# Ranking edges with first places in the last row of the marks, and 16-bit marks and frames laid out by fours in the first deal

## The reference

```python
h = relu(layernorm(x)); x = x + L0(h)   # mean of h[src] over the edges of each dst, then two 128x128 products
h = relu(layernorm(x)); x = x + L1(h)   # per-type weighted sums over dst, three products
h = relu(layernorm(x)); x = x + L2(h)   # attention with 4 heads over the edges of each src, with edge attributes
h = relu(layernorm(x)); x = x + segment_sum(h[dst], src)
```

## Time and profile before

| | us |
|---|---|
| median of 3 runs (11649.42 to 11655.3) | 11650.15 |
| the profiled execution | 11690.42 |
| its span | 11688.7 |
| second ranking loop, turn 0, inside 91 to 265 | 174 |
| second ranking loop, turn 1, inside 341 to 515 | 174 |
| first deal, 556 to 1250 | 694 |
| from 1260 to 11680 | 10420 |

### The profile page before, as it was taken

One profiled execution on the slowest core, in us unless ns is written; L12 is line 12 of the kernel. 1 busy time (PEld: TensorE's weight loads), 2 busy tenths in 40 slices (PEclk: granted clock), 3 DMA queues, 4 the chain that ended last, 5 costly groups with the idle time before them and its releaser, 6 DMA issues. The chain is left out here.

```text
span 11688.7 us, 111903 instructions
## 1 busy us (share of the span) xinstructions
PE 6256.4 (54%) x29027; PEld 4853.4 (42%) x29027; DVE 6469.5 (55%) x14870; ACT 2647.0 (23%) x8519; POOL 6742.7 (58%) x7099
## 2 busy tenths in 40 slices
PE   8744577777775355555554455555555333333333
PEld 2233455555554333333333455555555333333333
DVE  7799766666664455555554555555555622233223
ACT  0033111111110244444442243444444300000000
POOL 0055566666665566666665455555555466666665
PEclk6555788888887676666666777877777655555555
DMA  0000233333334422222222333333333322222223
GB/s 26 12 10 10 56 76 73 76 76 76 76 75 86 110 46 46 47 47 46 47 46 31 85 85 87 87 87 87 86 87 88 65 46 47 48 47 47 47 47 53
DMA packets 1413627, 706.78 MB, mean 60 GB/s; under 512 B 1170036, under 2 KB 1273944, under 8 KB 1412872
## 3 DMA queue, kind: packets, MB, share of 16 engines
q0 software_dynamic: 254160, 559.07, 19.0%
q1 hardware_dynamic: 1158840, 140.57, 8.6%
HBM read 595.05 MB, written 104.05 MB: 60 GB/s over the span
## 5 line engine op out<-in xcount | busy, mean ns | idle before, releaser
L1042 POOL DMA_INDIRECT l_rows<-h_tab,l_index x1616 | 1525.7, 944 | 942.3 <-issue 452.8
L1425 POOL DMA_INDIRECT l_rows<-h_tab,l_index x1616 | 1527.7, 945 | 868.5 <-issue 472.5
L603 POOL DMA_INDIRECT l_rows<-h_tab,l_words x1616 | 1524.6, 943 | 828.2 <-issue 461.8
L646 PE MATMUL l_sums<-l_onehot,l_rows 128*128 128x128 f32 x3232 | 829.5, 438 | 1599.0 <-issue 875.5
L1560 PE MATMUL l_sums<-l_weighted,l_rows 128*128 128x256 f32 x3232 | 1199.0, 537 | 712.7 <-DVE acc L1487 673.6
L646 PEld LDWEIGHTS l_sums<-l_onehot,l_rows 128*128 128x128 f32 x3232 | 719.6, 328 | 1708.9 <-issue 1076.1
L1947 PE MATMUL l_ps_q<-qtab,h 128*128 x3232 | 831.4, 413 | 1099.6 <-ACT h L1836 783.9
L634 DVE TENSOR_TENSOR acc<-acc,l_sums 128x128 f32 x1616 | 462.6, 286 | 1646.4 <-remote 733.8
L1439 ACT ACTIVATE l_weighted<-l_onehot,l_weights 128x128 f32<-128x128 bf16 x3232 | 987.5, 388 | 1427.2 <-DVE l_onehot L554 1084.1
L1487 DVE TENSOR_TENSOR acc<-acc,l_sums 128x256 f32 x1616 | 677.4, 419 | 1047.8 <-remote 687.4
L759 PE MATMUL src_sums<-tmp 128*128 128x288 f32 x3128 | 1042.2, 486 | 401.8 <-DVE tmp L736 217.7
(11 more groups left out here) (345 smaller groups left out, 11296.6 us busy)
## 6 DMA issues: line engine op xcount, KB each, us to landing
staged<-tmp SPq DMA_DIRECT2D x391, 152.0 KB
l_rows<-h_tab,l_index POOLq DMA_INDIRECT x3232
l_rows<-h_tab,l_words POOLq DMA_INDIRECT x1616
by_src<-words_src SPq DMA_DIRECT2D x96, 152.0 KB
l_kv<-kv_tab,l_words POOLq DMA_INDIRECT x816
l_attr<-in_edge_attr SPq DMA_DIRECT2D x44, 272.0 KB
l_kv<-kv_tab,moments POOLq DMA_INDIRECT x600
h_tab<-h SPq DMA_DIRECT2D x21, 448.0 KB, 3.0
```

The costliest lines, as they stand in the source:

```text
L603: pool.indirect_dma_start(rows[b][:, j, :], None, table, bass.IndirectOffsetOnAxis(ap=words[k % 3][:, at + j, 0:1], axis=0)).then_inc(rows ...
L646: done = nc.tensor.matmul(sums[q % SUMS][:, j, 0:P], rows[b][:, j, :], onehot[b][:, j, :], start=True, stop=True)
L1042: pool.indirect_dma_start(rows[b][:, j, 0:D], None, table, bass.IndirectOffsetOnAxis(ap=index[q // Q16 % WORDS][:, q % Q16 * H + j, :], ax ...
L1425: pool.indirect_dma_start(rows[b][:, j, :], None, h_tab, bass.IndirectOffsetOnAxis(ap=index[q // Q16 % WORDS][:, q % Q16 * H + j, :], axis ...
```

## The change

Ranking, second loop. The row 127 of each mask no longer holds a mask. It is overwritten by a DMA of the row of `start` for this bin, and `before` gets ones in its last row, so that one matmul adds both parts: four matmuls a bin in place of eight. Masks, `before`, `twice` and `zeros16` become float16, there are BINS_AHEAD = 4 masks, two of them in room of `h`, and `offer` and copy_predicated run on 127 rows. The edges of row 127 are placed apart: PE picks their bins (`from_last`), DVE makes `row_eq` and `row_sel` from them and from `row_value`, and at the end of the loop eight matmuls (`last_row`, `last_lift`) and one addition over 32 partitions (`tail`) bring their places into `chunk`.

First deal. `chunk`, `first` and `opened` are copied once to bfloat16, padded; a table of numbers 1 to 128, each repeated four times, is made by POOL, and DVE copies its bits into the PSUM table. Marks become `[P, GB, P, GC]` and frames `[BINS, P, GB]`: the innermost run is four neighbouring columns or deals of one number. Operands and output of these comparisons are then 16-bit values with step one. PE reads weights with a step of four elements (8 bytes).

```diff
+BINS_AHEAD = 4
+BLOCKS = -(-DEALS // GB)
+PADDED = BLOCKS * GB + 4
...
+                for turn in range(2):
+                    sp.wait_ge(start_ready, turn + 1)
+                    for b in range(NB):
+                        t = b % BINS_AHEAD
+                        if b >= BINS_AHEAD:
+                            sp.wait_ge(mask_used, turn * NB + b - BINS_AHEAD + 1)
+                        sp.dma_start(onehot[t][P - 1:P, :], start[b:b + 1, :]).then_inc(start_row_ready[t], 16)
                 sp.wait_ge(zeroed, ZEROS)
...
+                keep_where(before[:], ALU.not_equal, 1.0, 1 - P, [[0, P]])
+                for table, value in ((last_row, 1.0), (last_lift, K - 1.0)):
+                    ch.link(nc.gpsimd.memset(table[:], 0.0))
+                    ch.link(nc.gpsimd.memset(table[0:NB, P - 1:P], value))
...
-                ch.link(nc.gpsimd.memset(only[:], 0.0))
-                keep_where(only[:], ALU.not_equal, 1.0, 0, [[-1, BINS]])
...
+                    ch.link(nc.vector.scalar_tensor_tensor(by_group(start[:]), of_group, float(K), by_group(cnt), ALU.mult, ALU.add))
+                    nc.vector.scalar_tensor_tensor(by_group(row_value), of_group, float(K), by_group(run), ALU.mult, ALU.add).then_inc(start_ready, 1)
...
                     def offer(b):
-                        nc.vector.tensor_scalar(onehot[b % 2][:], bins_of[:], bins[:, b:b + 1], None, ALU.is_equal).then_inc(oh_ready[b % 2], 1)
+                        nc.vector.tensor_scalar(onehot[b % BINS_AHEAD][0:P - 1, :], bins_of[0:P - 1, :], bins[0:P - 1, b:b + 1], None,
+                                                ALU.is_equal).then_inc(mask_ready, 1)
...
+                    for b in range(BINS_AHEAD):
+                        offer(b)
+                    dve.wait_ge(row_bins_ready, turn + 1)
+                    dve.wait_ge(start_ready, turn + 1)
+                    ch.link(nc.vector.tensor_scalar(row_eq.rearrange("p (c q) -> p c q", c=4), banks[0][0:BINS, :, 0:CQ], bin_no[:, 0:1], None,
+                                                    ALU.is_equal))
+                    nc.vector.tensor_tensor(row_sel, row_value, row_eq, ALU.mult).then_inc(row_sel_ready, 1)
...
+                    dve.wait_ge(row_found, turn + 1)
+                    tail = chunk[P - 32:P, :].rearrange("p (c q) -> p c q", c=4)
+                    ch.link(nc.vector.tensor_tensor(tail, banks[1][P - 32:P, :, 0:CQ], tail, ALU.add))
...
+                    pe.wait_ge(row_sel_ready, turn + 1)
                     for b in range(NB):
...
+                        pe.wait_ge(mask_ready, turn * NB + b + 1)
+                        served = len(range(t, NB, BINS_AHEAD))
+                        pe.wait_ge(start_row_ready[t], 16 * (turn * served + b // BINS_AHEAD + 1))
                         if n:
                             pe.wait_ge(slot_used[s], turn * SERVED[s] + n)
                         for c in range(4):
-                            nc.tensor.matmul(banks[s][:, c, 0:CQ], before[:], onehot[s][:, cut], start=True, stop=False)
-                            last = nc.tensor.matmul(banks[s][:, c, 0:CQ], only[:, b:b + 1].to_broadcast([BINS, P]), start[:, cut], start=False, stop=True)
-                        last.then_inc(oh_used[s], 1)
+                            last = nc.tensor.matmul(banks[s][:, c, 0:CQ], before[:], onehot[t][:, c * CQ:(c + 1) * CQ], start=True, stop=True)
+                        last.then_inc(mask_used, 1)
+                    pe.wait_ge(slot_used[1], (turn + 1) * SERVED[1])
+                    for c in range(4):
+                        nc.tensor.matmul(banks[1][:, c, 0:CQ], last_row[:], row_sel[:, cut], start=True, stop=False)
+                        last = nc.tensor.matmul(banks[1][:, c, 0:CQ], last_lift[:], row_eq[:, cut], start=False, stop=True)
+                    last.then_inc(row_found, 1)
...
+    def lay(self, dve):
+        nc = self.nc
+        for to, of, n in ((self.chunk16, self.chunk, EC), (self.first16, self.first, DEALS + 1), (self.opened16, self.opened, DEALS)):
+            nc.vector.tensor_copy(to[:, 0:n], of[:, 0:n]).then_inc(self.laid, 1)
+            nc.vector.memset(to[:, n:], 0.0).then_inc(self.laid, 1)
+        dve.wait_ge(self.numbered, 1)
+        numbers = self.numbers[:].rearrange("p j c -> p (j c)").bitcast(F32)
+        nc.vector.tensor_copy(self.words_of_numbers, numbers).then_inc(self.laid, 1)
+        dve.wait_ge(self.laid, 7)
...
-        iota = self.iota[0:BINS, :].unsqueeze(1).to_broadcast([BINS, n, P])
-        of = lambda table, at: table[:, at:at + n].unsqueeze(2).to_broadcast([BINS, n, P])
-        nc.vector.tensor_tensor(self.left[b][:, 0:n, :], iota, of(self.opened, lo), ALU.is_equal)
+        iota = self.iota16[0:BINS, :, :]
+        of = lambda table, at: table[:, at:at + GB].unsqueeze(1).to_broadcast([BINS, P, GB])
+        nc.vector.tensor_tensor(self.left[b][:], iota, of(self.opened16, lo), ALU.is_equal)
...
+    def mark_chunks(self, m, lo, n):
+        size = [P, GB, P, GC]
+        chunks = self.chunk16[:, lo * GC:(lo + GB) * GC].rearrange("p (g c) -> p g c", c=GC)
+        self.nc.vector.tensor_tensor(self.onehot[m % 2][:], self.iota16.unsqueeze(1).to_broadcast(size), chunks.unsqueeze(2).to_broadcast(size),
+                                     ALU.is_equal)
+
+    def onehot_of(self, m, column):
+        return self.onehot[m][:, column // GC, :, column % GC]
+
+    def framed_of(self, table, i):
+        return table[:, :, i]
```

More of the change, by code:

```diff
@@ L256, in rank_phase @@
         start = sb("start", [BINS, EC], F16)
+        last_row, last_lift, bin_no = sb("last_row", [BINS, P], F16), sb("last_lift", [BINS, P], F16), sb("bin_no", [BINS, 1])
+        from_last = sb("from_last", [P, BINS], BF16)
+        halves_of_a = room[0:BINS, 2 * EC:3 * EC].bitcast(F16)
+        row_eq = halves_of_a[:, 0:EC]
+        row_value, row_sel = room[0:BINS, 0:EC], room[0:BINS, 3 * EC:4 * EC].bitcast(F16)[:, 0:EC]
         bins = sb("bins", [P, BINS])
-        only = sb("only", [BINS, BINS], F16)
-        twice = sb("twice", [P, 2 * BINS], BF16)
+        twice = sb("twice", [P, 2 * BINS], F16)
         lower = sb("lower", [BINS, BINS])
@@ L682, in wide @@
             return room[:, at:at + n].rearrange(f"p ({' '.join(names)}) -> p {' '.join(names)}", **dict(zip(names[1:], sizes[1:])))
-        self.onehot = [wide(f"onehot{b}", [span * GC, P]) for b in range(2)]
+        if dt != BF16:
+            self.onehot = [wide(f"onehot{b}", [span * GC, P]) for b in range(2)]
         self.filled = [wide(f"filled{b}", [span * GC, K * carried]) for b in range(2)]
@@ L686, in __init__ @@
         self.out = [wide(f"out{r}", [K, carried + self.ints]) for r in range(RING)]
-        frame = lambda name: sb(name, [BINS, GB, P], BF16)
-        self.left, self.next = ([frame(f"{name}{b}") for b in range(2)] for name in ("left", "next"))
+        if dt != BF16:
+            frame = lambda name: sb(name, [BINS, GB, P], BF16)
+            self.left, self.next = ([frame(f"{name}{b}") for b in range(2)] for name in ("left", "next"))
         ps = lambda name: own.enter_context(nc.psum_tensor(f"{tag}_{name}", [P, 512], F32))
@@ L751, in tensor @@
                 pe.wait_ge(self.move_kept, g)
-            nc.tensor.matmul(self.moves[:, 0:P], self.left[k][:, i, :], self.next[k][:, i, :], start=True, stop=True).then_inc(self.moved, 1)
+            nc.tensor.matmul(self.moves[:, 0:P], self.framed_of(self.left[k], i), self.framed_of(self.next[k], i),
+                             start=True, stop=True).then_inc(self.moved, 1)
         if g >= 2:
@@ L758, in tensor @@
         for c in range(GC):
-            last = nc.tensor.matmul(sums, self.onehot[m][:, at + c, :], self.filled[m][:, at + c, :].rearrange("p (k w) -> p k w", k=K),
+            last = nc.tensor.matmul(sums, self.onehot_of(m, at + c), self.filled[m][:, at + c, :].rearrange("p (k w) -> p k w", k=K),
                                     start=(c == 0), stop=(g == 0 and c == GC - 1))
@@ L809, in __init__, with number @@
         self.shift, self.trash = shift, trash
-        frame = lambda name: own.enter_context(nc.sbuf_tensor(f"{tag}_{name}", [BINS, GB, P], BF16))
+        sb16 = lambda name, shape: own.enter_context(nc.sbuf_tensor(f"{tag}_{name}", list(shape), BF16))
+        frame = lambda name: sb16(name, [BINS, P, GB])
+        self.left, self.next, self.closed = ([frame(f"{name}_of{b}") for b in range(2)] for name in ("left", "next", "closed"))
         self.begun, self.beyond = frame("begun"), frame("beyond")
-        self.closed = [frame(f"closed{b}") for b in range(2)]
+        self.onehot = [sb16(f"onehot_of{b}", [P, GB, P, GC]) for b in range(2)]
+        self.numbers = sb16("numbers", [P, P, GC])
+        self.chunk16, self.first16, self.opened16 = sb16("chunk16", [P, BLOCKS * GB * GC]), sb16("first16", [BINS, PADDED]), sb16("opened16", [BINS, PADDED])
         self.rows = own.enter_context(nc.sbuf_tensor(f"{tag}_rows", [P, RING], I32))
```

(11 more changed lines are left out.)

78 lines of the change are left out of this document (47 added, 31 removed).

## The result

After the change the median is 11542.67 us (4 runs, 11536.17 to 11552.14), before it is 11649.78 in the same comparison: a ratio of 0.9908, 95% interval 0.9895 to 0.992. The kernel is 107 us faster; 268 were forecast, and the time lies outside the range. The profiled execution of after has a span of 11534.4.

What follows compares the result with a forecast made beforehand. PE was taken to bound the ranking loop and DVE the first deal, POOL after the change. Ranking -79.2, deal -188.9 and +0.5 for its start sum to -267.6 us: median 11382.5 us, range 11362 to 11482.

Steps and rivals of the forecast that it cites:

- Ranking, -79.2: Second ranking loop, both turns: four matmuls fewer a bin, DVE sets the pace at 2.53 us, less additions: -79.2 us.
- Rows of `start`, 0: Ranking loop: PE's added wait for 49 single-row DMAs a turn stays hidden in 8.3 us of room, costing 0.
- rival 4: Ranking loop: rows of `start` land late, 12.3 us, so the loop gains nothing; 11481 us, chance 0.05.
- DVE's block, 4.93: First deal: 16-bit marks and frames at 0.52 ns an element cut DVE's block from 7.07 to 4.93 us.
- Rival 1: First deal: 16-bit comparisons reading PSUM don't run at twice the rate, block stays 7.07 us; 11573 us, chance 0.10.
- Strided weights: First deal: PE's weight loads of every fourth 16-bit element keep full speed; PE with ACT stays 0.77 us a deal.
- rival 2: First deal: strided weight loads slow PE, doubled loads giving 11511 us; case covers 11420 to 11573, chance 0.08.
- rival 3: First deal: strided loads far slower, four times the duration, whole kernel slower than before, about 12170 us; chance 0.03.
- Their second sign: First deal: DVE and POOL both idle for PE, named beside weight loads over 0.2 us as showing rivals 2 or 3.
- What is late next. POOL: First deal becomes bound by POOL's indirect DMAs, 1.27 us apart; first to last issue 685.4 to 496.5 us, -188.9.
- The ring: First deal's four output buffers: landing stays hidden, 3.3 us against 5.09 until the same buffer's turn.
- I see no path but the clock: The 10420 us of unchanged work after the first deal would not move by themselves, except through the clock.

Runs made afterwards that it cites:

- rank_alone: Only the change's ranking half, first deal as in before; median 11611.27 us, ratio to before 0.9925.
- flat16: The changed kernel with 16-bit operands kept but marks and frames laid out row by row again; median 11614.3 us, ratio to before 0.9929.
- laid32: The changed kernel with the layout by fours kept but marks and frames compared from 32-bit operands again; 11616.09 us in one run.

## Why the prediction was wrong in one term

- **Ranking, -79.2: right.** Measured -85.4 with the entry to the deal, -87 by `rank_alone`. A bin takes 2.47 where 2.53 was worked out, the additions a little less.
- **Rows of `start`, 0: right** (the earlier trace rows was a sound guide); rival 4 did not occur.
- **DVE's block, 4.93: nearly.** 5.03, the one frame at the odd offset being 0.13 dearer. Rival 1 did not occur: with one operand in PSUM the marks ran at nearly twice the old rate (1208 ns in place of 2276 for 2048 elements). That settles for this case the two pages of the Trainium skill that the prediction set against each other. VectorE: DVE Perf Modes, "The perf-mode tier table", would have had the single rate for an operand in PSUM, and the measurement is against it; Vector Engine (DVE) Microarchitecture Reference, "Performance modes", asks for two-byte types with step one in all operands, and both 1208 ns and `flat16`'s 2276 (a repeated scalar has step zero) agree with it.
- **Strided weights: right.** 126 ns in place of 120 for the marks' loads in after, and 127 in `laid32`; so rivals 2 and 3 did not occur. Their second sign, DVE and POOL both idle for PE, did show, which the prediction had tied to slow loads alone.
- **"What is late next. POOL", -188.9: this is the step that failed.** It measured -38.2. The working took PE with ACT at 0.77 us a deal and ACT's 1.5 us wherever in POOL's burst a deal fell, and put DVE's wait for PE at 0.15 us a block. But the earlier trace rows shows two deals at the start of a block, one just ahead of POOL's burst at 803.22 and one just behind its first issue, and half of before's carry signals rose there, most of the others behind the burst. The faster DVE brought PE's work into the bursts, where under the held condition 160 of 170 signals reached ACT late; DVE's wait for PE became 1.5 us a block, 144.3 in all, and took back most of the gain. POOL is the bound in the free condition alone, and there the term is right: 499.8 us measured, 496.5 worked out. That the whole gain of 268.5 there lies within 1 us of the forecast is partly luck: up to the first issue it was 7 us better than worked out, the row of issues 3 us worse, and no free profile of before says how the rest divides.
- **The ring** was to stay hidden, with 3.3 us against 5.09. In the held condition eight buffers were no better than four, and in the free one four cost 3 us.
- **"I see no path but the clock"** for the 10420 us behind was right for this change, but the rows of those stages held the warning: "remote" was the leading reason of DVE's and ACT's waits for PE there, and half to four fifths of PE's signals came late there. That indirect DMAs are the reason in those stages too is likely, but was tried in the first deal alone.
- **The range** took in rival 4 and the nearer part of rival 2, and none of the four rivals was a wait for PE that grows while PE itself is no slower. The result (11543) lies between rival 2's 11511 and rival 1's 11573, but by neither mechanism.

No version beats the changed kernel by more than can be measured: eight buffers are 0.06% faster in the free condition, and in the held one a deal takes as long with eight (1.65 us) as with four (1.60).

## What to carry to other kernels

A stage that shows a handover at one phase only (here the first two deals of a burst) gives no price for that handover at other phases; before moving work there, look for the same handover in stages that use all phases, and read "remote" as a wait that the other engine's work does not explain. The 16-bit comparison of two tensors on VectorE got its double rate here only where every operand's innermost run was of neighbouring 16-bit elements; a repeated scalar lost it, a run of four neighbours that is repeated kept it. Measure the kernel before beside every experiment: compared with the earlier after alone, a deeper ring would have passed for the cure here, and only before, itself 1700 us faster in that set, showed that it was none.

## What the runs showed of the hardware that was not expected

- TensorE's completion signals can be held back, 0.5 to 4.6 us in the first deal of after, and then rise together (801.43, and two more within 0.09 us), under a condition of the chip that all kernels measured together share, and that two chips had in one set and not in another. Under it the whole kernel takes some 1700 us more of 11650: from the deal's last issue to the end 10408 to 10448 us, against 8676 to 8702 in the free one (PE's granted clock there is 0.79 in place of 0.71, so not all of it need be signals).
- In the first deal it goes with indirect DMAs of POOL's queue that follow each other at 1.27 us (64 to 70 of some 147 signals late in 80 deals); with plain DMAs of the same queue 1 of 163 and 0 of 162 were late, with plain and indirect ones in turn 0 of 143. What holds the signals, and what makes the condition, these runs do not show, nor whether spacing the indirect DMAs would cure it.
- An odd offset of a 16-bit operand made a comparison of 512 elements 535 ns in place of 405 (lines 913 and 911).
